# Two copies of the transposed normalised rows on VectorE instead of ScalarE, and one more wait on GpSimd, in a Mamba and gated-MLP layer

## The reference, cut to what matters

```
xi, z = split(W_in x)                                   # 512 channels each
u  = silu(conv4(xi) + conv_b)                           # 4 taps along the tokens
dbl = W_xproj u;  dt = softplus(W_dt dbl[:16] + b_dt);  B, C = dbl[16:32], dbl[32:48]
h[t] = h[t-1] * exp(dt[t] A) + (dt[t] u[t]) B[t]        # 512 channels x 16 states
y[t] = sum_s h[t, s] C[t, s];  y = (y + u D_skip) * silu(z)
x1 = layernorm(x + W_out y)
out = layernorm(x1 + W_down(silu(W_gate x1) * (W_up x1)))
```

## Time and profile before

| what | value |
|---|---|
| runs | 1801.61, 1802.52 and 1809.47 us; median 1802.52 us |
| the profiled execution | 1808.44 us, of which the span from first to last instruction is 1806.7 us |
| mean granted TensorE clock | 0.989 of full speed |
| PE matmul busy | 1738.0 us (96% of the span) |
| ACT busy | 1712.5 us (95%) |
| DVE busy | 1683.7 us (93%) |
| POOL busy | 1482.0 us (82%) |
| x1T copies on ACT | 30 instructions, 19.4 us, 649 ns each |
| tap steps on DVE | 189 instructions, 163.9 us, 888 ns each |

### The profile page before, as it was taken

The page is one execution under the profiler, slowest core; times in us unless marked ns, Lnnn a source line. Parts: engine busy times, 40 slices in busy tenths (PEclk is TensorE's granted clock), DMA queues, the critical chain, the costliest instruction groups (busy, mean ns, idle before and its releaser), DMA issues.

```text
span 1806.7 us, 40364 instructions
## 1 busy us (share of the span) xinstructions
PE 1738.0 (96%) x15678; PEld 1216.0 (67%) x15678; DVE 1683.7 (93%) x1970; ACT 1712.5 (95%) x2907; POOL 1482.0 (82%) x852
## 2 busy tenths in 40 slices
PE   7778999999999999999999999999999999999997
PEld 3455676766767676676767767676676767667676
DVE  5999999999999999999999999999999999999974
ACT  6898999999999999999999999999999999999971
POOL 5896897979979798997979979797997979889850
PEclk9899999999999999999999999999999999999999
DMA  7040130303113040131303013040221304022000
GB/s 210 1 120 1 4 118 15 118 1 86 47 16 117 13 120 2 18 115 15 118 2 103 29 15 118 14 119 1 47 86 15 118 1 126 7 38 83 1 24 24
DMA packets 171487, 100.57 MB, mean 56 GB/s; under 512 B 139408, under 2 KB 157584, under 8 KB 163232
## 3 DMA queue, kind: packets, MB, share of 16 engines
q1 hardware_dynamic: 171296, 97.98, 18.8%
HBM read 88.52 MB, written 9.44 MB: 54 GB/s over the span
## 4 chain that ended last, share of the span: by engine, by line
PE 41%; ACT 24%; DVE 11%; issue 11%; POOL 11%; SPq 0%; DMA 0%; ACTq 0%; POOLq 0%; DVEq 0%
PE ring L1160 14%; PE tp L1139 11%; POOL drive L568 9%; ACT decay L704 8%; ACT hT L711 7%; DVE h L915 7%; PE yb L1153 6%; PE ring L1252 4%; DVE acc L936 2%; PE ring L1228 2%; PE ring L1197 1%; ACT acc L720 1%; ACT L741 1%; ACT yt L732 1%; POOL diag_c L576 1%
## 5 line engine op out<-in xcount | busy, mean ns | idle before, releaser
L568 POOL TENSOR_TENSOR drive<-dtu,b_all 128x1024 f32<-128x1024 f32 x511 | 1208.4, 2396 | 8.6 <-DVE h L915 5.7
L704 ACT ACTIVATE decay<-dt,a_neg 128x512 f32<-128x512 f32 x1024 | 705.4, 718 | 15.7 <-DVE h L915 14.9
L915 DVE TENSOR_TENSOR_SCAN h<-decay,h,drive 128x512 f32<-128x512 f32 x512 | 620.2, 1267 | 9.6 <-ACT decay L704 6.5
L1139 PEld LDWEIGHTS tp<-ident,h 128*128 128x128 f32 x4096 | 463.4, 141 | 238.2 <-issue 124.0
L915 DVE TENSOR_TENSOR_SCAN h<-decay,drive 128x512 f32<-128x512 f32 x512 | 592.3, 1209 | 28.6 <-ACT decay L704 25.7
L711 ACT ACTIVATE hT<-tp 128x512 f32<-128x512 f32 x1024 | 595.5, 618 | 13.3 <-PE tp L1139 12.3
L1139 PE MATMUL tp<-ident,h 128*128 128x128 f32 x4096 | 563.2, 277 | 36.3 <-ACT hT L711 28.0
L1153 PE MATMUL yb<-hT,diag_c 128*32 128x128 f32 x8192 | 275.7, 277 | 7.1 <-ACT yt L732 5.2
L1153 PEld LDWEIGHTS yb<-hT,diag_c 128*32 128x32 f32 x8192 | 210.8, 110 | 82.7 <-issue 48.2
L1160 PE MATMUL ring<-xt,w_in 128*128 128x512 f32 x512 | 245.1, 602 | 2.3 <-ACT acc L752 2.3
L936 DVE SCALAR_TENSOR_TENSOR acc<-xi,cw,acc 128x512 f32<-128x512 f32 x189 | 163.9, 888 | 14.5 <-ACT xi L722 10.6
(11 more groups left out here) (132 smaller groups left out, 1647.8 us busy)
## 6 DMA issues: line engine op xcount, KB each, us to landing
b_all<-bc_scratch SPq DMA_DIRECT2D x63, 1024.0 KB, 6.8
xt<-in_xT SPq DMA_DIRECT2D x16, 512.0 KB, 4.3
res<-in_x SPq DMA_DIRECT2D x16, 512.0 KB, 6.2
out<-res SPq DMA_DIRECT2D x15, 512.0 KB, 2.9
c_col<-bc_scratch SPq DMA_DIRECT2D x256, 2.0 KB, 2.4
bc_scratch<-dbl SPq DMA_DIRECT2D x16, 64.0 KB, 1.6
b_all<-bc_scratch SPq DMA_DIRECT2D x2, 512.0 KB, 4.5
w_g<-in_w_gT SPq DMA_DIRECT2D x1, 768.0 KB, 7.1
```

What stands on the lines that cost most here:

```text
L568: tt(drive[:, j % 4, :, :], src, b_all[:, n:n + 2, :], ALU.mult).then_inc(g_dr, 1)
L704: act(decay[decay_slot(k.parity, i)][:, :], dt[:, cb, :], ACT.Exp, scale=a_neg[:, cb, n:n + 1]).then_inc(a_da, 1)
L915: nc.vector.tensor_tensor_scan(h[:, h_slot(k.parity, q), at:at + T, i % 4], decay[decay_slot(k.parity, i)][:, :], drive[:, (i // 2) % 4, i ...
L1139: last = nc.tensor.transpose(tp[g % 2][:, b * P:(b + 1) * P], h[:, h_slot(k.parity, q), t0:t0 + TS, :].rearrange("p t s -> p (t s)"), iden ...
```

## The change

The copies of `x1T` 0 and 1 leave ScalarE's tables and stand on VectorE: in chunks 1 to 14 at (5,3), between `conv(0,1)` and `conv(1,0)`, in chunk 15 at (4,3), behind scan 19. They are `tensor_copy` instead of an activation with Copy. The semaphore `a_x1T` is named `x1T_kept`, with the same counts. GpSimd gets an item `yield` at (4,0), behind drive unit 8: it waits until one tap step of chunk k+1, which is `conv(0,0)`, is done.

```diff
 ACT_SIDE
-    (5, 3): [("hT", 15), ("hT", 16), ("xi", 2), ("xi", 3), ("hT", 17), ("x1T", 0), ("hT", 18), ("x1T", 1)],
+    (5, 3): [("hT", 15), ("hT", 16), ("xi", 2), ("xi", 3), ("hT", 17), ("hT", 18)],
 DVE_SIDE
-    (5, 3): [("max", 1), ("norm", 0), ("conv", 0, 1), ("conv", 1, 0), ("conv", 1, 1), ("conv", 2, 0), ...
+    (5, 3): [("max", 1), ("norm", 0), ("conv", 0, 1), ("x1T", 0), ("x1T", 1), ("conv", 1, 0), ("conv", 1, 1), ...
 POOL_SIDE
-    (3, 0): [("gate", 3), ("diag", 1)], (3, 1): [("std", 1)], (4, 1): [("diag", 2)], (5, 0): [("diag", 3)],
+    (3, 0): [("gate", 3), ("diag", 1)], (3, 1): [("std", 1)], (4, 0): [("yield", 0)], (4, 1): [("diag", 2)], (5, 0): [("diag", 3)],
 ACT_LAST
-    (4, 1): [("hT", 14), ("hT", 15)], (4, 3): [("z", 3), ("hT", 16), ("x1T", 0), ("x1T", 1), ("hT", 17)],
+    (4, 1): [("hT", 14), ("hT", 15)], (4, 3): [("z", 3), ("hT", 16), ("hT", 17)],
 DVE_LAST
-    (4, 1): [("norm", 0)], (5, 3): [("gs", 0)], (6, 1): [("gs", 1)],
+    (4, 1): [("norm", 0)], (4, 3): [("x1T", 0), ("x1T", 1)], (5, 3): [("gs", 0)], (6, 1): [("gs", 1)],
 GpSimd, item()
+                if what == "yield" and head:
+                    wait(eng, v_conv, conv_steps(k + 1, 1))
 ScalarE
-            def copy_x1T(k, dh):
-                wait(eng, p_x1T, k.count(2, dh + 1))
-                act(xt[:, (k.parity + 1) % 2, dh, :], bank(k, "x1T", dh)[:, :], ACT.Copy).then_inc(a_x1T, 1)
 VectorE
+            def copy_x1T(k, dh):
+                wait(eng, p_x1T, k.count(2, dh + 1))
+                nc.vector.tensor_copy(xt[:, (k.parity + 1) % 2, dh, :], bank(k, "x1T", dh)[:, :]).then_inc(x1T_kept, 1)
```

More of the change, by code:

```diff
@@ L85 @@
     (2, 1): [("skip", 3)], (3, 3): [("conv", 0, 0), ("r1", 0)], (4, 2): [("r1", 1)],
-    (5, 3): [("max", 1), ("norm", 0), ("conv", 0, 1), ("conv", 1, 0), ("conv", 1, 1), ("conv", 2, 0), ("conv", 2, 1), ("conv", 3, 0), ("conv", 3, 1)],
+    (5, 3): [("max", 1), ("norm", 0), ("conv", 0, 1), ("x1T", 0), ("x1T", 1), ("conv", 1, 0), ("conv", 1, 1), ("conv", 2, 0), ("conv", 2, 1), ("conv", 3, 0), ("conv", 3, 1)],
     (6, 0): [("gs", 0), ("gs", 1)], (6, 2): [("hid", 0)], (7, 0): [("gs", 2)], (7, 1): [("hid", 1)],
@@ L417, in mamba_ffn @@
         a_sz = sem("a_sz"); a_xb = sem("a_xb"); a_dbl = sem("a_dbl"); a_e = sem("a_e"); a_ln = sem("a_ln")
-        a_y = sem("a_y"); a_x1T = sem("a_x1T"); a_th = sem("a_th"); a_o = sem("a_o"); a_set = sem("a_set")
+        a_y = sem("a_y"); x1T_kept = sem("x1T_kept"); a_th = sem("a_th"); a_o = sem("a_o"); a_set = sem("a_set")
         v_h = sem("v_h"); v_x1 = sem("v_x1"); v_y = sem("v_y"); v_conv = sem("v_conv"); v_dt = sem("v_dt")
@@ L810, in item @@
                     normalise(k + -2)
-                if what == "x1T" and tail:
-                    copy_x1T(k + -1, i)
                 if what == "tanh" and tail:
@@ L868, in end_x1T @@
                 act(of_half(k, s), end_bank(end_place["x1T", s])[:, :].rearrange("p (a t) -> p a t", a=DH),
-                    ACT.Copy).then_inc(a_x1T, 1)
+                    ACT.Copy).then_inc(x1T_kept, 1)
             def end_tanh(k, p, s):
@@ L982, in rest_of_layer @@
                     normalise(k)
+                if what == "x1T":
+                    copy_x1T(k, i)
                 if what == "gs":
@@ L1171, in left @@
                     "out": (v_r1, k.count(2, n + 1)),
-                    "x1T": (a_x1T, k.count(2, n + 1)),
+                    "x1T": (x1T_kept, k.count(2, n + 1)),
                     "gate": (v_gs, k.count(6, n + 1)),
@@ L1240, in gate_up @@
                 if m == 0:
-                    wait(eng, a_x1T, k.count(2, 2))
+                    wait(eng, x1T_kept, k.count(2, 2))
                 x1 = xt[:, (k.parity + 1) % 2, :, :]
@@ L1350, in end_gate_up @@
                 if before[0] == "x1T":
-                    eng.wait_ge(a_x1T, k.count(2, before[1] + 1))
+                    eng.wait_ge(x1T_kept, k.count(2, before[1] + 1))
                 if before[0] == "gate":
@@ L1355, in end_gate_up @@
                     eng.wait_ge(e_hid, 3 * before[2] + before[1] + 1)
-                eng.wait_ge(a_x1T, k.count(2, s + 1))
+                eng.wait_ge(x1T_kept, k.count(2, s + 1))
                 weight, done = (w_g, e_gate) if what == "gate" else (w_u, e_up)
```

## The result

The changed kernel takes 1844.39 us (median of 4 runs, 1843.99 to 1847.23), the kernel before 1805.47 us in the same comparison: ratio 1.0212, 95% interval 1.0186 to 1.0237. It is slower, as forecast, but by more: 36 us between the two profiled executions where the sum had 22, and 39 us between the medians where the forecast of 1830 had 27.5. It lies outside the range, which ended at 1838.

The account below looks back on a forecast made before the run. A closed loop through ScalarE, VectorE's block, `heads` and `tanh` 0 was taken as the bound. Copies +29.4, chunk 15 +1.0, stall -8.2 gave +22.2 us on 1808.44, 1830.6; forecast 1830, range 1818 to 1838.

Parts of the forecast that it names:

- The loop over VectorE's block: ScalarE's chunk, decay 23, scan 23, VectorE's max, norm and tap steps, `heads`, `tanh` 0 form a closed loop; slack 0.09 us.
- ScalarE's relief is worth nothing: Removing about 1.1 us of copies a chunk only makes ScalarE wait at `tanh` 0, gated by `heads`.
- The copy's price: Each 128x512 PSUM copy advances VectorE by 0.60 us; the faster SBUF row would give 0.32.
- Standing still for the second transpose: In chunk 7 VectorE waits for `x1T` 1, making conv(1,0) 2.28 us late: 1.2 copying, 1.1 standing still.
- Against this stand the slack of 0.09 at `tanh` 0 and about 0.1 more: Slack at `tanh` 0 and TensorE's relative earliness reduce the 2.3 us lateness to 2.1 us a chunk.
- TensorE gains a few tenths there, and loses them at `up` 0: Earlier `y` 0 helps TensorE at `sum` 4; `up` 0, behind `gs` 0 with 0.3 us slack, takes it back.
- The wait on GpSimd: The yield removes the long tap step in chunk 1, 8.2 us less; priced at 0 in the other chunks.
- The base: Profiled 1808.44 us read as having the chunk-1 stall, two lower runs without; median then goes to 1833, otherwise 1824.7.
- Chunk 15: Copies behind scan 19 make scan 20 start 1.85 us late; cost taken as 1.0 us, between 0 and 1.9.

Follow-up runs that it names:

- e5: Changed kernel with the copies behind conv(1,0) and `x1T` 1 in front of `sum` 3 on TensorE; 1815.18 us, ratio 1.0053.
- e3: Changed kernel with both VectorE copies one tap step later, behind conv(1,0); 1824.55 us, ratio 1.0095.
- e4: Changed kernel with TensorE doing `x1T` 1 in front of `sum` 3 instead of behind it; 1826.23 us, ratio 1.0104.
- e7: Changed kernel with TensorE repeating the four transposes of group 23 five times in chunks 1 to 14, filling its gap; 1834.49 us, ratio 1.0157.
- e6: Changed kernel with both copies left out in all chunks but the end stage, the wait on GpSimd kept; timing only, 1799.19 us.
- e10: Kernel before with the wait on GpSimd in front of drive 8 instead of behind it, copies on ScalarE; 1816.22 us, ratio 1.0058.
- e2: Changed kernel without the wait on GpSimd, the copies alone; 1853.4 us, ratio 1.026.
- e1: Kernel before with the wait on GpSimd alone, copies still on ScalarE; 1800.69 us, ratio 0.997.
- e8: Changed kernel with `u` 2 and the copy of states 22 moved in front of `tanh` 0 on ScalarE; 1841.65 us, ratio 1.0202.

## Why the prediction was wrong

The sum had 22.2 us, measured are 36.0. Of the 13.8 between them about 8.2 are the clock in six chunks, 3.6 the block in chunks 2 to 14, 3.3 the clock in front of chunk 1; chunks 1 and 15 give 0.3 and 1.1 back. Without the 8.2 the result would be 1836 us, inside the range.

First the loop, as means of chunks 2 to 14, the block taken from the start of the second tap step to the end of the last:

| kernel | block us | period us |
|---|---|---|
| before | 8.24 | 107.78 |
| e5 | 9.32 (+1.07) | 108.84 (+1.06) |
| e3 | 9.83 (+1.59) | 109.38 (+1.60) |
| e4 | 10.05 (+1.80) | 109.60 (+1.82) |
| e7 (the changed kernel's block, no lower clock) | 10.62 (+2.37) | 110.17 (+2.39) |

- *The loop over VectorE's block* was right: in the changed kernel each of its links has its new wait, and each microsecond in the block is one of the period.
- *ScalarE's relief is worth nothing*: right (e6).
- *The copy's price*: 0.69 us and 0.61 of advance, against 0.60. The Trainium skill's rule that a float32 operand in PSUM stays at the plain rate ("VectorE: DVE Perf Modes", section "Why PSUM operands drop a tier") is borne out by that row: 0.61 us, not the 0.32 of the faster row.
- *Standing still for the second transpose*: right. The second copy starts 3.19 us behind the second tap step in chunk 7, by the forecast 3.18. The wait shows as 0.91 instead of 1.1 us because the copy in front of it took its full 0.69.
- *"Against this stand the slack of 0.09 at `tanh` 0 and about 0.1 more"*: mis-sized, the second term that failed. 2.1 us were taken, 2.38 measured, 3.6 us over 13 chunks. By the table the means show none of the 0.2 us of slack. In chunk 7 `tanh` 0 starts 0.50 us behind the last tap step before the change and 0.51 behind it after: there the 0.09 us between `heads` and `tanh` 0 is part of the path. In chunk 6 it comes closer by 0.13 us (0.54 to 0.41), and that chunk grew by 2.32 instead of 2.36 us. `up` 0 does come 0.25 us nearer to the block's end (2.13 to 1.88 us), but that is TensorE's loop, and ScalarE's keeps its length.
- *"TensorE gains a few tenths there, and loses them at `up` 0"*: this is the step that failed. It named the place and put what TensorE does behind the new pause at nothing, without a reason. Six times 1.37 us = 8.2 us came from the granted clock (e7). The trace of before had a case to read it from: 5.83 us for 16 products behind the 6.50 us wait in chunk 1, where the same products take 3.62 in the changed kernel. That pause is longer than 2.3 us, so it could give a rival with a price, not a forecast. The Trainium skill ("TensorE: Matmul & The Clock Gate", section "HAM oscillation — how this bites in real kernels") tells of a kernel whose waits of about 3 to 5 us between bursts of products send the clock down in every round. The trace agrees in kind, not in size: here the pauses are 2.2 to 2.5 us, and the clock falls behind 6 of 14.
- *The wait on GpSimd*: right in chunk 1 (6.4 us less, with the block's 2.3 against it) and 0 elsewhere. The Trainium skill's rule that the loser of the shared ports waits for one instruction ("SBUF — State Buffer", section "SBUF: two separate sides") fits `max` in e10, which ends 1.1 us behind drive 12, and the steady tap steps of 1.55 us, which end 0.5 us behind drive 8. It doesn't fit the 9.3 us in chunk 1 of before and of e2.
- *The base*: right. The profiled execution was one with the stall, as read; by the groups about half of before's runs are. e1, the kernel without the stall and with the copies on ScalarE, takes 1800.69 us, and the forecast cost of the copies, 29.4 + 1.0, on top of it gives 1831. So the miss lies in the copies and the clock, not in the base.
- *Chunk 15*: right, though the -0.1 of the first table hides it. Between executions with the same clock the copies cost 1.3 us, against 1.0 forecast; that the profiled one shows nothing is chance, 3.41 us at the lower clock instead of 6.83.

## What to carry to other kernels

With three engines above 90%, ask where the engine that is relieved waits next and where the engine that is loaded stands in the order, not which has more free time: the same two copies cost 1.1, 1.6 or 2.4 us a chunk by the places of two entries in the tables. To test such a loop, lengthen the block by several amounts and plot the period against it: a slope of one from the first tenth says that there is no slack. A wait that becomes visible on TensorE costs more than its length when the granted clock falls behind it; look in the trace of before for a pause of that kind and read what the next products took. A stall that appears in some executions only shows as two groups of times, and the profiled one may belong to either. Before a stage's difference is put down to the change, compare its stretches at the lower clock: here about 3 us in front of chunk 1 and 1.3 us in chunk 15 went with them, where the change had no part.

## What the runs showed of the hardware

- TensorE idle for 2.2 to 2.5 us once a chunk was followed by the lower clock in 6 of 14 chunks (7 of 14 in e2, 5 of 14 in e8), for 3.41 us each, at 1.37 us of period each. The fall came between 0.1 us before the end of the pause and 1.4 us behind it. Behind pauses of 1.4 to 1.7 us (e3) and 1.3 to 1.6 us (e4) it never came, in 28 chunks. What decides between the chunks with the same pause isn't shown.
- A tap step with both inputs in SBUF took 9.32 and 9.33 us while GpSimd ran five instructions one behind another, and ended half a microsecond behind the fifth; in other chunks it ended half a microsecond behind the first. In the two long cases it started 0.2 us behind the start of GpSimd's drive, in the others 1.3 to 1.4 us behind it. No semaphore connects the two, so the engines meet at more than semaphores. Why it isn't let in between the five stays open.
